# A chunk's bounding factor ahead of the next chunk's exponential, and in SBUF

## The reference

```
def step(h, inp):
    xt, dt, bt, ct, t = inp
    dA = jnp.exp(jnp.clip(dt[..., None] * A, -10.0, 0.0))
    dBx = dt[..., None] * bt[:, None, :] * xt[..., None]
    h = dA * h + dBx
    hn = jnp.clip(jnp.linalg.norm(h, axis=-1, keepdims=True), 1e-06, None)
    scale = jnp.where(hn > 10.0, 10.0 / hn, jnp.ones_like(hn))
    h = jnp.where(t % 16 == 15, h * scale, h)
    y = jnp.einsum('bn,ben->be', ct, h) + D_param * xt
    return (h, y)
```

## Time and profile before

| | us |
|---|---|
| median of three runs | 5128.81 (5125.25 to 5131.53) |
| the profiled execution's own time | 5127.9 |
| its span in the profile | 5126.1 |
| VectorE busy | 4168.0 (81% of the span) |
| TensorE busy, matmuls | 4429.8 (86%) |
| ScalarE busy | 2860.8 (56%) |
| POOL busy | 2685.7 (52%, all of it in the first 3450 us) |
| mean granted TensorE clock | 0.944 |

### The profile page before, as it was taken

One profiled execution on the slowest core, in us unless ns is written; L12 is line 12 of the kernel. 1 busy time (PEld: TensorE's weight loads), 2 busy tenths in 40 slices (PEclk: granted clock), 3 DMA queues, 4 the chain that ended last, 5 costly groups with the idle time before them and its releaser, 6 DMA issues.

```text
span 5126.1 us, 83699 instructions
## 1 busy us (share of the span) xinstructions
PE 4429.8 (86%) x22592; PEld 3113.2 (61%) x22592; DVE 4168.0 (81%) x9876; ACT 2860.8 (56%) x8386; POOL 2685.7 (52%) x1412
## 2 busy tenths in 40 slices
PE   5789888888989888888989888887677679999999
PEld 4667767776767767676767767743343434444444
DVE  4999999999999999999999999973333447777777
ACT  5777777777777777777777777734444420000000
POOL 3888777777888777777888778850000000000000
PEclk8999999999999999999999999998898889999999
DMA  2111111111111111111111111101010100000000
GB/s 88 56 46 50 44 55 44 52 48 51 48 45 50 45 54 44 52 48 51 48 45 50 45 54 44 49 26 48 25 49 25 39 26 18 18 18 18 18 18 16
DMA packets 119407, 214.07 MB, mean 42 GB/s; under 512 B 19232, under 2 KB 85664, under 8 KB 118560
## 3 DMA queue, kind: packets, MB, share of 16 engines
q1 hardware_dynamic: 119072, 211.10, 12.4%
HBM read 184.83 MB, written 26.21 MB: 41 GB/s over the span
## 4 chain that ended last, share of the span: by engine, by line
PE 38%; issue 28%; DVE 26%; ACT 3%; POOL 2%; DVEq 1%; DMA 1%; SPq 1%; POOLq 0%; ACTq 0%
PE ps L631 22%; DVE macc L954 5%; PE ps L758 2%; DVE ms L926 2%; PE ps L661 2%; PE ps L608 2%; PE ps L737 2%; PE ps L668 2%; DVE hb L868 2%; DVE xcv L1068 1%; DVE dtt L1119 1%; PE ps_dA L758 1%; DVE zt L1079 1%; DVE selp L914 1%; POOL prod L349 1%
## 5 line engine op out<-in xcount | busy, mean ns | idle before, releaser
L631 PE MATMUL ps<-w_x,mxT 128*128 128x512 f32 x4096 | 1882.0, 598 | 13.1 <-DVE macc L954 13.0
L349 POOL TENSOR_TENSOR prod<-hb,cbc 128x1024 f32<-128x1024 f32 x512 | 1121.7, 2191 | 461.7 <-DVE hb L870 448.7
L851 DVE TENSOR_TENSOR_SCAN hb<-ps_dA,hb 128x1088 f32<-128x1088 f32 x512 | 1240.3, 2423 | 60.5 <-issue 52.5
L414 ACT ACTIVATE zr<-dt,aneg 128x128 f32<-128x128 f32 x4096 | 1240.7, 388 | 40.8 <-DVE dt L997 40.8
L608 PE MATMUL ps<-prod,ident 128*128 128x128 f32 x8192 | 1050.9, 291 | 234.8 <-POOL prod L349 234.8
L608 PEld LDWEIGHTS ps<-prod,ident 128*128 128x128 f32 x8192 | 1033.0, 207 | 347.0 <-POOL prod L349 286.5
L357 POOL TENSOR_TENSOR hb<-u,bbc 128x1024 f32<-128x1024 f32 x512 | 1199.0, 2342 | 84.1 <-POOL prod L349 72.1
L631 PEld LDWEIGHTS ps<-w_x,mxT 128*128 128x128 f32 x4096 | 738.6, 191 | 708.3 <-issue 664.3
L954 DVE SCALAR_TENSOR_TENSOR macc<-ps,gate,macc 128x256 f32<-128x256 f32 x2048 | 978.4, 478 | 224.2 <-PE ps L631 161.9
L423 ACT ACTIVATE ps_dA<-zr 128x1024 f32<-128x1024 f32 x512 | 516.9, 1010 | 0.0
L430 ACT ACTIVATE sq<-hb 128x64 f32<-128x64 f32 x512 | 158.6, 310 | 342.4 <-DVE hb L851 342.1
(11 more groups left out here) (185 smaller groups left out, 5508.9 us busy)
## 6 DMA issues: line engine op xcount, KB each, us to landing
bbc<-bcd SPq DMA_DIRECT2D x128, 512.0 KB, 3.7
cbc<-bcd SPq DMA_DIRECT2D x128, 512.0 KB, 3.6
xt<-in_x SPq DMA_DIRECT2D x128, 128.0 KB, 3.1
x2d<-macc SPq DMA_DIRECT2D x64, 128.0 KB, 1.7
xcv<-x2d SPq DMA_DIRECT2D x64, 128.0 KB, 2.1
x3d<-x1b SPq DMA_DIRECT2D x64, 128.0 KB, 1.9
x1b<-x3d SPq DMA_DIRECT2D x64, 128.0 KB, 2.0
out_dram<-macc SPq DMA_DIRECT2D x64, 128.0 KB, 1.7
```

The costliest lines, as they stand in the source:

```text
L349: TT(dst, states, cc, ALU.mult).then_inc(M["prodp"], 1)
L414: last = act(zr[k][:, s, :], dt[:, s // N, :], ACT.Relu, bias=10.0, scale=aneg[:, s:s + 1])
L631: last = mm(banks[p % len(banks)][:], mxT[k][:, j, :], w_x[:, j, p * 512:(p + 1) * 512], start=(j == 0), stop=(j == KD - 1))
L851: V.tensor_tensor_scan(states, dA, states, 0.0, ALU.mult, ALU.add).then_inc(M["scan"], 1)
```

## The change

ScalarE's two rows of `norms` for chunk c go ahead of the exponential of chunk c + 1 (or of the next tile's chunk 0), and the factor `nf` becomes an SBUF tensor of its own.

```diff
+        nf = sb("nf", [P, EB])
...
-        nf = trio[:, ST * SL + 16:ST * SL + 16 + EB]
...
-                act(nf, nrl[:], ACT.Exp, scale=-0.5, bias=math.log(10.0)).then_inc(M["ne"], 1)
+                act(nf[:], nrl[:], ACT.Exp, scale=-0.5, bias=math.log(10.0)).then_inc(M["ne"], 1)
...
                     if S_:
                         squares(i, c)
+                    if S_:
+                        norms(i, c)
                     if S_ and c < NC - 1:
                         exponentials(i, k, c + 1)
                     elif G_ and c == NC - 1:
                         exponentials(i + 1, 1 - k, 0)
-                    if S_:
-                        norms(i, c)
...
-                factor = nf.rearrange("p (e t) -> p e t", t=1).broadcast_to([P, EB, N])
+                factor = nf[:].rearrange("p (e t) -> p e t", t=1).broadcast_to([P, EB, N])
```

## The result

| | before | after |
|---|---|---|
| median of four runs, us | 5130.17 (5125.25 to 5132.70) | 5248.64 (5243.42 to 5248.75) |
| ratio to before, 95% interval | | 1.0230 (1.0212 to 1.0247) |
| span of the profiled execution, us | 5126.1 | 5241.6 |
| VectorE busy, us | 4168.0 | 4286.6 |
| mean granted TensorE clock | 0.944 | 0.936 |

What follows compares the result with a forecast made beforehand. VectorE sets the pace; the tile's end follows POOL's unbroken run from L373. Delays of 0.64 + 0.97 and 0.25 in that run gave 1.85 us per tile, over 61 tiles 113 us on 5127.9: 5241 us, range 5210 to 5275.

Steps and rivals of the forecast that it cites:

- What bounds the kernel: VectorE sets the pace, hardly waits for the factor; the tile's end follows L501, L373, POOL's unbroken run of 12.94 us, L936.
- Part 1: Factor in SBUF: L868 and L870 (the pair) wait for POOL; its product is +0.34 late after chunk 1, +0.64 after chunk 3.
- the first rival: At L868 and L870, the port costs nothing; only ScalarE's order costs, 61 us, 5189 us; chance 0.20.
- the case I had named as costing the same: Chunk 1: if L868 slipped in ahead of POOL's L366, L870 would pay the +1.07 us wait instead.
- Part 2: ScalarE's order: in chunk 5 the moved exponential stands between factor and sigmoid, +0.97 us; other chunks costed at nothing.
- the 0.3 us that I had set for the case: Later exponential in chunk 1 and squares in chunk 2: up to 0.3 us per tile if the covering waits are gone.
- Part 3: Both delays meet at L501, 1.6 us later; POOL's run grows about 0.25 at chunk 6: L936 +1.85 us per tile.
- Sum: Over the scan, 61 of 64 tiles × 1.85 = 113 us, added to 5127.9: 5241 us.
- The rival in which waits add up: L1031 and its like in chunk 4 swallow nothing: 3.1 us per tile, 190 us, 5318 us; chance 0.13.
- The third rival: At the tile's end VectorE gets ahead of POOL's last L357: −1.1 us per tile, −69 us, 5059 us; chance 0.07.
- The fourth: On ScalarE the exponential's delay is swallowed too, and L868 and L870 cost nothing: no change; chance 0.05.

Runs made afterwards that it cites:

- the second and third experiment: Changed kernel with ScalarE's old order in chunk 5 alone: 5194.14 us; changed kernel with the new order in chunk 5 alone: 5248.33 us.
- the first experiment: Changed kernel with ScalarE's order put back, so only the factor in SBUF remains: 5190.69 us, ratio 1.0116.
- the edit of the tile's end: L926, L936, L1107 made one-element tensor_scalar operations, L939 and L942 moved behind L1119: 5082.18 us on the kernel before, 5218.03 on the changed one.
- the fastest version: Kernel before with L926, L936, L1107 as tensor_scalar, L939 and L942 behind L1119, and POOL's L373 behind chunk 5's product: 5034.78 us.

## Why the prediction was right

**What bounds the kernel** held. Making the factor ready earlier gained nothing, because VectorE had not been waiting for it, and the tile's end followed POOL's run: of 1.32 us put ahead of the sigmoid, with nothing else touched, 1.20 came out in the tile.

**Part 1** held in its mechanism and was a little small. The pair waits for the POOL instruction in flight, although the factor is a broadcast of four values, so the first rival fell. The delay of POOL's product is +0.37 after chunk 1 (forecast 0.34) and +0.81 after chunk 3 (0.64), measured on the clock set by each tile's previous L870. Most of the missing 0.17 lies at chunk 3: L370 starts 0.38 late, not 0.3, and L870 starts 0.05 after L370's end, where I had it 0.06 before. In chunk 1 it was L868 that slipped in ahead of L366 and L870 that paid, the case I had named as costing the same. For that case I had cited the earlier trace rows, which do not show it: L357 starts there 0.17 us behind L349, as it does elsewhere, and so need not have waited. The rows of chunk 1 show it: L366 lasts 1.39 us instead of 1.28, since it waits for L868, and still goes ahead of L870. The means came out the other way round, L868 at 0.37 and L870 at 0.40 us, where I had 0.5 and 0.34.

**Part 2** held: +0.95 against 0.97, and chunk 5 alone carries it, as the second and third experiment show. The other chunks were rightly costed at nothing while the pair's wait covers them. Where POOL's pieces were moved and that cover is gone, they cost more than the 0.3 us that I had set for the case: in the tile shown VectorE waits 0.17 us ahead of chunk 2's scan for the exponential and 0.51 ahead of its reduce for the squares.

**Part 3**: L373 starts 1.77 late where I had 1.6. In chunk 6 I had L870 behind L378; in the timeline it is L378 that waits (0.83 us long, not 0.73). POOL's run grew by 0.10, not 0.25. The two misses nearly cancel, which was luck: 1.77 + 0.10 = 1.87 for a forecast 1.85.

**Sum**: two tiles take 108.39 us from one L997 to the next but one (1643.23 to 1751.62), against 104.76 in the kernel before (1591.72 to 1696.48), 1.82 per tile. In the mean of tiles 4 to 59 a tile went from 52.41 to 54.20 us, 1.79 more: 0.76 up to the reduce of chunk 5 (forecast 0.64), 0.94 from there to L373 (0.97) and 0.08 in POOL's run (0.25). From the first L851 to the last the scan takes 113 us more (83.3 to 3514.1, against 83.6 to 3401.4), as much as the 61 × 1.85 of the forecast; but that is 1.77 over all 64 tiles, so the low count of tiles and the high price of one cancel, which was luck again. The forecast was 5241, the median is 5248.64. The experiments split it into 60 us for the place and 58 for the order.

The rival in which waits add up fell for the reason given against it: POOL is later too, so L1031 and its like swallow the difference. The third rival, VectorE ahead of the last L357, did not come about: L936 lasts over 2.1 us in every one of tiles 4 to 59. The fourth, no change, fell with the first experiment and with the one of the two more exponentials.

## What to carry to other kernels

A row that is long for its shape may be waiting inside; compare it with the same line where the other engine is idle (L936 took 0.15 us there, 2.3 here). The pair waited for a running POOL instruction with both inputs in SBUF, and never with one in PSUM, so an operand in PSUM can be worth more than it seems; and a wait that was taken from one row was mostly paid by another. Rows that read one tensor and scalars waited too (L1067 1.88 us where it takes 0.41 alone, L939 1.26 where it takes 0.35), while L926 as a one-element `tensor_scalar` took 0.21 us in all its 128 executions. An exponential that ran while its engine would have waited anyway was free; behind that wait it cost only in chunk 5, where another engine's long run starts from what comes next.

## What the runs showed of the hardware that was not expected

- The pair is not shorter with the factor in SBUF: the median row is 264 ns for L868, 257 with the factor in PSUM. The estimate from the Trainium skill (VectorE: DVE Perf Modes, section on the TRN2 errata) of 65 ns less for an SBUF source does not show for this shape, whose other input is strided.
- ScalarE's four-column Exp takes 206 ns into SBUF and 177 into PSUM, in every execution.
- VectorE's idle time at the loop's turn grew with the edit of the tile's end: 52.5 to 79.8 us over 28 turns in the kernel before, 49.9 to 95.9 in the changed one. In the fastest version, whose tiles are shorter still, it is 79.7. What VectorE waits for there no row shows; it stays open.
- In one stretch of the kernel before with fewer rows that wait for POOL, TensorE had idled 2.91 us ahead of L661 and then had a granted clock of 0.55 for 7 us, near its lower level of 1.2 GHz, in the row by stretch below (the clock is third from the end); eight L661 then took 3.78 us, against 1.99 in the kernel before at 1598.46. VectorE waited for TensorE's convolution 1.40 us in that tile, but only twice in 2000 us, so it does not carry the result.

```profile
1630.00:1637.00 7.00, 6.82 (x15) 4.31 (x16) 6.80 (x11) 6.37 (x20) 6.79 (x4) 0.55 0.00 1
```
